# Loading four pairs of the next sample early, and reading four channels fewer a second time

## The reference

```
for the depthwise layers:
    pooled  = x.mean(axis=(2, 3)); hdn = relu(pooled @ w1 + b1)
    kernels = (hdn @ w2 + b2).reshape(b, 32, 3, 3)
    out     = depthwise 3x3 convolution of x with kernels, padding 1
x = x + out
```

## Time and profile before

| | us |
|---|---|
| median of three runs | 4175.83 |
| lowest, highest | 4156.57, 4193.7 |
| the profiled execution's own time | 4194.23 |
| its span | 4192.4 |
| TensorE busy | 3239.0 (77%) |
| VectorE busy | 2184.1 (52%) |
| ScalarE busy | 1696.8 (40%) |
| GpSimd busy | 1899.0 (45%) |
| DMA, ScalarE's queue (q10): 359.81 MB | 28.9% of the 16 engines' span |
| DMA, SyncE's queue (q1): 467.67 MB | 49.2% of the 16 engines' span |

### The profile page before, as it was taken

How to read it: one execution, slowest core, us unless ns; L and a number is a source line. 1 busy time by engine, 2 the same in 40 slices (tenths; PEclk the granted TensorE clock), 3 DMA queues, 4 the chain that set the end, 5 groups by cost and what they waited for, 6 DMA issues and landing times.

```text
span 4192.4 us, 70846 instructions
## 1 busy us (share of the span) xinstructions
PE 3239.0 (77%) x26592; PEld 2052.9 (49%) x26592; DVE 2184.1 (52%) x6326; ACT 1696.8 (40%) x2466; POOL 1899.0 (45%) x3167
## 2 busy tenths in 40 slices
PE   0676988769877698867987779867888769877698
PEld 0453555435554355644555445554455535555355
DVE  1627844277432874328743386434854258532772
ACT  1442733336333363434634345343543436334233
POOL 1326544165542554426543454524645155442654
PEclk9998999889998899988999889988999889998899
DMA  7278888887979779797895977969789697896946
GB/s 218 53 126 194 192 290 241 144 179 190 309 214 152 174 204 303 201 172 179 219 300 170 202 165 227 287 157 215 174 250 295 113 215 186 259 289 119 192 77 227
DMA packets 611739, 846.05 MB, mean 202 GB/s; under 512 B 492227, under 2 KB 492998, under 8 KB 578630
## 3 DMA queue, kind: packets, MB, share of 16 engines
q1 hardware_dynamic: 311104, 467.67, 49.2%
q10 hardware_dynamic: 251142, 359.81, 28.9%
q0 software_dynamic: 49152, 14.05, 2.0%
HBM read 452.84 MB, written 267.45 MB: 172 GB/s over the span
## 4 chain that ended last, share of the span: by engine, by line
PE 49%; DMA 17%; DVE 14%; SPq 6%; issue 5%; ACT 5%; ACTq 3%; POOL 0%; DVEq 0%; POOLq 0%
PE acc L1061 27%; PE acc L1078 16%; DMA signs<-arena 5%; DVE dense_stats L930 5%; DMA dense_out<-arena 4%; DMA arena<-signs 4%; SPq L349 3%; PE acc L1140 3%; DVE y L941 2%; ACTq L594 2%; ACT arena L657 2%; ACT arena L642 2%; DMA arena<-dense_out 2%; SPq L451 2%; ACTq L664 1%
## 5 line engine op out<-in xcount | busy, mean ns | idle before, releaser
L1061 PE MATMUL acc<-y,arena 64*128 64x384 f32 x9216 | 1685.9, 492 | 49.2 <-ACT y L626 33.9
L1061 PEld LDWEIGHTS acc<-y,arena 64*128 64x128 f32 x9216 | 983.8, 190 | 602.3 <-ACT y L626 119.5
L626 ACT ACTIVATE y<-acc 128x768 f32<-128x768 f32 x896 | 697.5, 808 | 1282.4 <-PE acc L1078 1281.8
L1078 PE MATMUL acc<-arena 64*128 64x384 f32 x4608 | 963.1, 512 | 219.2 <-issue 197.0
L550 POOL TENSOR_SCALAR arena<-arena,cst,fill 128x24 f32<-128x24 f32 (+1 forms) x1536 | 620.2, 423 | 922.1 <-issue 652.3
L569 POOL TENSOR_TENSOR y<-arena,y 128x3072 f32<-128x3072 f16 x80 | 464.9, 5828 | 825.2 <-DMA arena<-dense_out 825.2
L1078 PEld LDWEIGHTS acc<-arena 64*128 64x128 f32 x4608 | 516.0, 196 | 459.8 <-issue 234.2
L930 DVE BATCH_NORM_STATS2 dense_stats<-y 128x6 f32<-128x192 f32 x1536 | 406.5, 345 | 626.6 <-POOL y L569 625.8
L1140 PE MATMUL acc<-arena,wd_side 128*32 128x384 fp8e4 (+1 forms) x10752 | 472.8, 331 | 288.5 <-DMA arena<-signs 233.9
L349 POOL DMA_DIRECT2D arena<-y x1024 | 529.3, 524 | 364.8 <-PE acc L1078 311.7
L1140 PEld LDWEIGHTS acc<-arena,wd_side 128*32 128x32 fp8e4 x10752 | 308.4, 102 | 473.5 <-issue 241.0
(11 more groups left out here) (89 smaller groups left out, 1410.6 us busy)
## 6 DMA issues: line engine op xcount, KB each, us to landing
out<-y ACTq DMA_DIRECT2D x128, 1152.0 KB, 13.7
y<-x ACTq DMA_DIRECT2D x112, 1152.0 KB, 32.7
arena<-x SPq DMA_DIRECT2D x147, 576.0 KB, 7.1
dense_out<-arena ACTq DMA_DIRECT2D x384, 192.0 KB, 6.9
arena<-dense_out SPq DMA_DIRECT2D x192, 384.0 KB, 6.8
arena<-y SPq DMA_DIRECT2D x512, 141.0 KB
arena<-signs SPq DMA_DIRECT2D x192, 250.0 KB, 10.3
signs<-arena SPq DMA_DIRECT2D x128, 312.5 KB, 3.5
```

The costliest lines, as they stand in the source:

```text
L626: nc.scalar.activation(y[:, 2 * g:2 * g + 2, k * KN:(k + 1) * KN], acc[:, 2 * k:2 * k + 2, 0:KN], ACT.Identity, accum_out=sums[:, g, k:k + ...
L1061: nc.tensor.matmul(acc[:, 2 * k + odd, 0:KN], w_center[at, slot, 2 * q + odd, :], y[at, 2 * g + odd, k * KN:(k + 1) * KN], start=turn == 0 ...
L1078: nc.tensor.matmul(acc[:, 2 * k + odd, 0:KN], w_halo[at, slot, q, :], halo[at, bt % HALO_SLOTS, q, k * KN:(k + 1) * KN], start=False, stop ...
```

## The change

The next sample's pairs 0 to 3 are now all loaded three pairs behind their stores (at pairs 3, 4, 5 and 6 of layer 3), where before only pairs 0 and 1 were; pairs 4 to 15 are loaded where they were. The eight channels of these four pairs get their statistics from `y`, at pairs 7, 8, 10 and 11. So 24 channels in place of 28 are read a second time. ScalarE's 16 and VectorE's 4 in layer 2 stay as many, but are other channels. Of the late readings four stay, used at pairs 0, 1, 2 and 4; three are issued before layer 3's loop and one in it, ahead of the halos of chunk 3. `clean_stage` follows the last late reading from chunk 5 to chunk 3 of GpSimd's loop, because its place hangs on `LATE_WITH[-1]`.

```diff
-AHEAD_FIRST = 4
+AHEAD_FIRST = 8
 AHEAD_ACT = [(AHEAD_FIRST + i, i % 2) for i in range(PAIRS)]
 AHEAD_WITH = [2, 6, 9, 13]
 AHEAD_DVE = [(AHEAD_FIRST + PAIRS + n, 2) for n in range(len(AHEAD_WITH))]
-AHEAD_LATE = [(AHEAD_FIRST + PAIRS + len(AHEAD_WITH) + n, (0, 2, 1)[n % 3]) for n in range(8)]
+AHEAD_LATE = [(AHEAD_FIRST + PAIRS + len(AHEAD_WITH) + n, (0, 2, 1)[n % 3]) for n in range(4)]
 AHEAD = AHEAD_ACT + AHEAD_DVE + AHEAD_LATE
 AHEAD_SLOTS = 3
-LATE_WITH = [0, 1, 2, 4, 5, 6, 8, 9]
-ARRIVE_WITH = 10
+LATE_WITH = [0, 1, 2, 4]
+ARRIVE_WITH = [7, 8, 10, 11]
@@ in depthwise of the vector block
                         if g in LATE_WITH:
                             ahead_stats(s, AHEAD_LATE[LATE_WITH.index(g)])
-                        elif ARRIVE_WITH <= g < ARRIVE_WITH + AHEAD_FIRST // 2:
-                            dve.wait_ge(loaded[g - ARRIVE_WITH], 16 * (s + 2))
-                            for c in (2 * (g - ARRIVE_WITH), 2 * (g - ARRIVE_WITH) + 1):
+                        elif g in ARRIVE_WITH:
+                            pair = ARRIVE_WITH.index(g)
+                            dve.wait_ge(loaded[pair], 16 * (s + 2))
+                            for c in (2 * pair, 2 * pair + 1):
                                 channel_stats(c, y[:, c], dve_ahead)
```

## The result

The changed kernel is a little faster: 4164.41 us median of 20 runs, against 4183.78 us of 20 runs of the kernel before on the same chip. The ratio is 0.9956, with a 95% interval from 0.9937 to 0.9975. So the gain lies between 0.25 and 1.3%, 10 to 53 us; 87.5 us had been forecast, and 4164 us lies outside the range that ended at 4150. The profiled execution took 4157.82 us.

A forecast was written before the change was run, and what follows sets the result against it. A DMA backlog with a hole bounds each transition; 11 us from layer 3 and 1 to 2 from layer 0, taken as 12.5, times 7 give 87.5 us, forecast 4088 us; range 4036 to 4148, rounded, ending at 4150.

The forecast's parts named there:

- The 11 us: Layer 3, each transition: saving forecast as 17.7 - 2.8 (halos) - 2.5 (means) - 1.4 (small waits, slower clock).
- The 12.4 us for a chunk of halos behind a chunk: Layer 3, SyncE's queue: time for one chunk's halos without a reading, taken by bytes from 20.8 us.
- not 0.4: Layer 3, pair 8: chunk 4's halos were forecast 0.4 us late for TensorE; 2.8 us for chunks 4 to 7.
- the 2.5 us at pair 12's means: Layer 3, pair 12: means forecast 2.5 us late because VectorE's statistics wait for loads.
- Rival 1's rule: DMAs from any engine interleave on the same 16 engines; both layer 3 stalls stay, 7 us gained, 4127 us, chance 0.18.
- the other: Engines take turns between queues with work, so a deeper ScalarE queue costs layer 3's halos nothing more, as the forecast assumed.
- The backlog ends 13.3 us sooner: DMA in layers 3 and 0: backlog 13.3 us shorter, layer 0 starting 11 us sooner and getting 1 to 2 us shorter.
- The bytes' term: DMA backlog: three readings fewer, 1.77 MB at 293 to 347 GB/s, worth 5.1 to 6.0 us.
- The hole's term: DMA in layer 3: share 0.74 for 30 us, counted as 7.8 us of unused capacity to be gained.
- layer 0 grew by what layer 3 lost: Sign in layer 0 that would make the prediction wrong altogether; no size or chance of its own.
- a change within 1%: Whole kernel: median within about 1%, 42 us or 6 us a transition, of before; chance 0.18.

The follow-up runs named there:

- e1: Kernel before with pairs 2 and 3 of the next sample loaded three pairs behind their stores, all eight late readings kept: ratio 1.0061 to before.
- e2: Kernel before with four late readings in place of eight, loads where they were, statistics of the last four channels left out: ratio 0.9961 to before.
- e3: Changed kernel with VectorE's statistics for the eight arriving channels taken from channels 30 and 31, so that no load is awaited: ratio 0.9936 to before.
- e4: Changed kernel without any late reading, statistics of the next sample's last four channels left out: ratio 0.9895 to before.
- e5: Changed kernel with stores of pairs 8 and 9, each sample but the last, cut to 96 of 2304 values a partition: ratio 0.9923 to before.
- v4: Changed kernel with pairs 4 to 15 loaded six pairs behind their stores in place of seven: ratio 0.9878 to before.

## Why the prediction was wrong

**Layer 3: nearly right in its sum, by luck, since errors cancelled.** The 11 us were 9.3 (two profiles each). The 12.4 us for a chunk of halos behind a chunk failed: I had divided 20.8 us by bytes between a reading and a chunk. It measured 22.3 us in the transition shown and 18 to 22 us on average in every kernel, with one reading or with none. Chunk 4's halos take 26.5 to 28.1 us from their first issue to the border in every kernel whose halos stay on SyncE's queue, and its three slots leave 23; chunk 4 is late by that. So pair 8 stands 5.3 to 5.6 us on average (7.2 in the transition shown) and not 0.4. Against that, the chunks behind it kept pace: chunk 5 followed after 14 us (18 before), chunks 6 and 7 after 12.4 to 12.9 us. And the 2.5 us at pair 12's means weren't there (0.5 in the transition shown). In the transition shown, the last load awaited was done at 2109.5, 81 us into layer 3 (75.9 forecast), but TensorE was later too, because of pair 8.

**Rival 1's rule and the other.** That the queue makes no difference held for chunk 4's halos once they were issued, 27 us with readings ahead or without; their issue came 3.7 us sooner without. That a deeper queue beside them costs nothing held for chunk 4 as well: 53.0 us with loads 2 and 3 late, 53.4 and 53.7 with them early. This is what the Trainium skill states in "DMA: Bandwidth & Descriptors", section "Queues, rings and completion order" (engines take turns between the queues that have work), and for chunk 4 the traces agree. It did not hold for chunk 5, where the early loads fill what had been a hole: 2.6 to 2.9 us more with the readings gone, 5.7 with all of them kept. Neither rule tells how long a chunk takes.

**The DMA's side: the step that failed.** "The backlog ends 13.3 us sooner", made of 7.8 us of hole and 5.1 to 6.0 us of bytes. Load 15 landed 4.3 us sooner after layer 3's start, while layer 0 began 9.3 us sooner; so layer 0 had more of the backlog, and not less. In the transition shown the full DMA share ended 8.6 us sooner after layer 3's start. The bytes' term is worth 0.8 us by the last part of load 15 (the readings dropped alone). By 14 of its 16 parts it is worth 5.7 us, as I had it. The hole's term, by the step from there to the changed kernel, is 3.5 us by the last part and 1.6 by the 14, and less than nothing alone. So the hole, a DMA share of 0.74, was worth less than half of the capacity that I had read in it, whichever way it is counted: the stretches after it had to carry the same two loads. The bytes' term was made of a mean over 16 engines, while the time, as argued next, goes by the parts that land last.

**Hence layer 0.** In the eight kernels whose halos stay on SyncE's queue and whose loads are whole (before, after, e1 to e5, v4), layer 0 ends 37.7 to 39.6 us after load 15, from the one with 241.2 us in both layers to the one with 231.0. After load 15's last part TensorE stands 4 us or less in layer 0, before it 16 to 19. The columns add up by their making, so that 4.3 us of load 15 and 1.8 of the rest are the 6.2 us measured and no proof of it. Load 15 is also issued in pair 6 of layer 0, 30 us before its landing in the kernel before and 34 after, and layer 0 ends 69 to 76 us after that issue in the same kernels; a steady distance alone doesn't tell cause from effect. What tells more is where layer 0's time went. Of TensorE's idle time there (waits over 0.3 us, on average), 11.7 us lay before the 14th part's landing, 5.1 between it and the last part's, and 1.7 behind that; in the changed kernel 10.0, 8.8 and 2.1. So the loss is in the stretch in which 14 parts are done, at a share of 0.4, and which went from 13 us to 16. That halos wait for the same late parts is how I read it; the trace doesn't tell which engine a packet ran on. For it: with the side halos on GpSimd's queue in layers 0 and 3 the stretch is 9.7 us and TensorE's idling in it 2.5. The two loads cut show that the tail counts: 7.4 us sooner, 4.3 us gained. The two stores cut are a case against it, 1.6 us sooner and nothing gained. I had named this outcome, "layer 0 grew by what layer 3 lost", as what would make me wrong altogether, and gave it no chance of its own; a third of layer 3's gain was paid back, and not all. The chance of a change within 1% was 0.18.

**Open.** Why dropping bytes of stores in layer 3 gained nothing; why the last of the 16 parts lands 13 to 16 us behind the 14th, and what made it more in the changed kernel.

## What to carry to other kernels

Where one queue's backlog runs over the border of two stages, forecast the landing of its last item first, and of the last part of it: a mean share over 16 engines hides those that are behind. Don't count a share below 1 as time to be had. The place of the bytes matters more than their number: 2.2 to 2.4 MB less gave 4.3 us as two loads at the queue's tail, 1.8 us as four readings on another queue, and nothing as two stores in the middle. Two edits that each seem useful can need each other: loads early alone cost 0.6%; with the readings gone, they took 4.4 us off layers 3 and 0.

## What the runs showed of the hardware

- A full DMA share says that all engines have something in hand, and not how much they move: 347 GB/s in 34 us of layer 3 before, 295 after, at shares of 1.00 and 1.01.
- Load 15's 14th part landed 13 us before its last in the kernel before and 16 us in the kernel after. In that stretch the DMA share was 0.4, and TensorE stood 5.1 and 8.8 us.
- The issue of a chunk's eight halo copies takes SyncE 6 us in a quiet stretch and up to twice that where the DMA share is high. In the kernel before (time, duration, eight issues each), ahead of layer 3 and 15 us into it (share 0.93):

```profile
2046.17 5.96 SPq L349 DMA_DIRECT2D arena<-y  x8
...
2072.32 12.78 SPq L349 DMA_DIRECT2D arena<-y  x8
```

  The share doesn't set it alone: in the kernel after, chunk 4's eight take 13.4 us on average, at shares of 0.8 to 1.0, and chunk 6's 7.0, at 1.0.
- The same bytes of left and right halos on GpSimd's queue: 4.7 us a transition less in the changed kernel and 1.6 in the kernel before, where the other queues are backed up; 12.3 us a layer more in layer 2.
